# A causal attention and expert layer on one core: values held back beside projections, x laid out across, and a down product in full height

## The reference

```python
qkv = (x @ w_qkv).reshape(B, S, 3, H, D)          # H = 16 heads, D = 32
q, k, v = qkv[:, :, 0], qkv[:, :, 1], qkv[:, :, 2]
q, k = _unit_norm(q), _unit_norm(k)               # t * rsqrt(sum(t*t) + 1e-6)
q = m * _apply_rope(q, cos, sin) + (1.0 - m) * q  # m = 1 for heads 0, 2, 4, ...
k = m * _apply_rope(k, cos, sin) + (1.0 - m) * k
logits = einsum('bshd,bthd->bhst', q, k) * q_gain[None, :, None, None]
attn = softmax(where(causal, logits, finfo.min))
y = einsum('bhst,bthd->bshd', attn, v).reshape(B, S, Dm) @ w_out
x = _layernorm(x + y)
# 8 experts of width 352, the best 2 for each token, weighted by their softmax score
g = silu(einsum('td,edh->teh', x, w_gate)) * einsum('td,edh->teh', x, w_up)
routed = einsum('teh,ehd,te->td', g, w_down, comb)
shared = silu(x @ sw_gate) * (x @ sw_up) @ sw_down    # width 704
out = _layernorm(x + routed + shared)
```

## Time and profile before

| | us |
|---|---|
| median of 3 runs | 1081.23 |
| lowest and highest | 1080.83, 1082.02 |
| span of the profiled execution | 1101.7 |
| PE busy in it | 1056.5 (96%) |
| DVE, ACT, POOL busy | 623.5, 543.4, 395.7 |
| PE busy with scores L1495, values L1545 on exponents | 188.4, 136.7 |
| PE busy with projections L1445 (three parts) | 57.8, 56.2, 55.4 |
| PE busy with down products L751 on hid_h | 66.3 |

### The profile page before, as it was taken

How to read it: one execution, slowest core, us unless ns; L and a number is a source line. 1 busy time by engine, 2 the same in 40 slices (tenths; PEclk the granted TensorE clock), 3 DMA queues, 4 the chain that set the end, 5 groups by cost and what they waited for, 6 DMA issues and landing times.

```text
span 1101.7 us, 17977 instructions
## 1 busy us (share of the span) xinstructions
PE 1056.5 (96%) x6171; PEld 753.5 (68%) x6172; DVE 623.5 (57%) x1094; ACT 543.4 (49%) x900; POOL 395.7 (36%) x323
## 2 busy tenths in 40 slices
PE   7799999999999999999999996899999999999996
PEld 6654656645566466643477674589999999998885
DVE  3578694896848777687688452232222222223776
ACT  3467776687767776778645410123222222221213
POOL 2232132321224222214342177082466664623430
PEclk9999999999999999999999998799999999999999
DMA  6444514463353624346163036253444443423443
GB/s 192 131 130 136 160 63 125 129 173 96 97 143 106 182 58 116 106 129 177 48 207 110 7 147 239 88 194 103 155 155 155 131 155 102 134 85 105 125 134 115
DMA packets 106097, 141.58 MB, mean 129 GB/s; under 512 B 12784, under 2 KB 57328, under 8 KB 106032
## 3 DMA queue, kind: packets, MB, share of 16 engines
q1 hardware_dynamic: 89664, 103.22, 31.9%
q10 hardware_dynamic: 11088, 20.19, 5.3%
q0 software_dynamic: 5280, 17.31, 4.8%
HBM read 84.59 MB, written 56.10 MB: 128 GB/s over the span
## 4 chain that ended last, share of the span: by engine, by line
PE 83%; ACT 6%; DVE 5%; issue 3%; POOL 1%; another core or an unknown queue 1%; DMA 0%; SPq 0%; ACTq 0%; DVEq 0%
PE scores L630 14%; PE scores L1495 12%; PE bank L1445 12%; PE bank L1545 9%; PE scores L704 7%; PE bank L618 7%; PE bank L751 6%; ACT probs L1647 4%; PE scores L529 4%; PE bank L1542 3%; PE scores L646 2%; DVE key_sum L1768 1%; PE scores L595 1%; PE bank L1474 1%; POOL wqkv_l L1845 1%
## 5 line engine op out<-in xcount | busy, mean ns | idle before, releaser
L1647 ACT ACTIVATE probs<-scores,shift_now 128x1024 f32<-128x1024 f32 (+3 forms) x296 | 273.6, 975 | 82.4 <-PE scores L1495 64.5
L1768 DVE TENSOR_TENSOR key_sum<-key_sum,probs 128x2048 f32<-128x2048 f32 (+1 forms) x96 | 204.1, 2126 | 53.8 <-PE bank L1545 18.8
L1495 PEld LDWEIGHTS scores<-q_stack,k_stack 96*128 96x128 f32 x640 | 104.6, 190 | 137.9 <-ACT probs L1647 71.5
L1495 PE MATMUL scores<-q_stack,k_stack 96*128 96x512 f32 (+3 forms) x640 | 188.4, 405 | 3.7 <-ACT probs L1647 3.4
L1545 PE MATMUL bank<-probs,v_sb 128*32 128x512 f32 (+3 forms) x1184 | 136.7, 534 | 0.0
L630 PE MATMUL scores<-ffn_w,xt_h 128*128 (+1 forms) x608 | 127.4, 331 | 0.0
L1217 POOL TENSOR_TENSOR ffn_w<-raw,ones 128x1408 fp32r<-128x1408 f32 (+4 forms) x36 | 72.1, 2013 | 134.1 <-PE bank L618 97.0
L630 PEld LDWEIGHTS scores<-ffn_w,xt_h 128*128 128x128 f32 x608 | 99.8, 189 | 7.7 <-issue 5.5
L704 PE MATMUL scores<-x1T_h,ffn_w 128*128 128x512 f32 x352 | 92.2, 396 | 9.2 <-DVE silu L1043 6.4
L1009 DVE TENSOR_TENSOR ht_l<-scores,ht_h 128x256 fp32r<-128x256 f32 x39 | 16.6, 425 | 145.8 <-ACT ht_h L833 145.8
L1524 POOL TENSOR_SCALAR_AFFINE_SELECT probs<-probs 128x512 f32<-128x512 f32 x40 | 43.0, 1077 | 151.4 <-ACT probs L1647 151.2
(11 more groups left out here) (243 smaller groups left out, 1726.8 us busy)
## 6 DMA issues: line engine op xcount, KB each, us to landing
q_stack<-turn_scratch SPq DMA_DIRECT2D x48, 256.0 KB, 3.9
k_stack<-turn_scratch SPq DMA_DIRECT2D x48, 256.0 KB, 4.2
x_sorted<-zeros SPq DMA_DIRECT2D x39, 256.0 KB, 2.9
y_sorted<-y_tile ACTq DMA_DIRECT2D x39, 256.0 KB, 2.6
x_tile<-x_sorted ACTq DMA_DIRECT2D x37, 256.0 KB, 2.7
turn_scratch<-turned_h SPq DMA_DIRECT2D x32, 256.0 KB, 2.0
turn_scratch<-turned_l SPq DMA_DIRECT2D x32, 256.0 KB, 2.0
raw<-w_gate SPq DMA_DIRECT2D x8, 704.0 KB, 5.5
```

What stands on the lines that cost most here:

```text
L1495: mm = nc.tensor.matmul(scores[:, p, hh, lo:CH], k_stack[0:3 * HD, h, j * P:(j + 1) * P], q_stack[0:3 * HD, i % 2, h, lo:CH], start=True, ...
L1647: nc.scalar.activation(exponents(g, slot)[:, 2 * p:2 * p + 2, lo:CH], scores[:, p, :, lo:CH], ACT.Exp, bias=shift_now[:, p:p + 1]).then_in ...
L1768: nc.vector.tensor_tensor(key_sum[:, :, lo:CH], key_sum[:, :, lo:CH], probs[:, slot % 4, :, lo:CH], ALU.add).then_inc(sum_dve, 1)
```

## The change

It has four parts.

1. **x laid out across.** The host passes x a second time with the features on the partitions (`x_across`), w_qkv grouped by heads and the rotation tables by partition. x is loaded straight into `xT_raw`; the 64 transposes of x, with `pe_turn_x`, are gone. w_qkv of a group comes in one transfer of 6 KB rows in place of three of 512 B pieces. The first low part of w is made by DVE in place of POOL. The opening's projections go round three banks of PSUM and wait for the copy of the projection three before.
2. **Values held back.** In an odd slot with a projection, PE leaves out the values of the slot before and makes them in the next slot, ahead of that slot's own.
3. **Tables.** Projections, normalise, rotate, turn and stack entries are moved, and the reading of the sums of chunk 1 is no longer put inside a normalise (`SUMS_INSIDE`).
4. **Down product of half 0.** The third chunk (64 rows) has its high rows in one half of the partitions and its low rows in the other of `hid_h`. Two matmuls of 128 rows, with high weights twice and then zero over low weights, replace three of 64 rows. The weights take an extra transfer of 128 KB and an extra copy on ACT; a DVE memset stands in place of a subtraction.

```diff
-PROJECT_AT = {(0, 0): -15, (0, 1): -14, (0, 2): -13, (0, 3): -12, (1, 0): -9, (1, 1): -7, (1, 2): -4, (1, 3): -3,
...
+PROJECT_AT = {(0, 0): -13, (0, 1): -12, (0, 2): -11, (0, 3): -9, (1, 0): -7, (1, 1): -5, (1, 2): -4, (1, 3): -3,
+              (2, 0): 1, (2, 1): 2, (2, 2): 3, (2, 3): 5, (3, 0): 7, (3, 1): 9, (3, 2): 11, (3, 3): 13}
-NORMALISE_AT = {(0, 0): -12, (1, 0): -4, (2, 0): 4, (3, 0): 11}
-ROTATE_AT = {(0, 0): -11, (1, 0): -3, (2, 0): 6, (3, 0): 13}
+NORMALISE_AT = {(0, 0): -9, (1, 0): -3, (2, 0): 5, (3, 0): 13}
+ROTATE_AT = {(0, 0): -8, (1, 0): -2, (2, 0): 6, (3, 0): 15}
...
-OPENING = [("x", 0), ("x", 1), ("p", 0), ("x", 2), ("p", 1), ("x", 3), ("x", 4), ("p", 2), ("x", 5), ("x", 6),
...
+OPENING = [("p", n) for n in range(9)] + [("t", 0), ("p", 9), ("t", 1), ("p", 10), ("p", 11), ("t", 2)]
...
+def held(g, slot):
+
+    return slot % 2 == 1 and any(True for _ in work_at(PROJECT, slot, g))
...
-                mm = nc.tensor.matmul(qkv_ps[:, 0:3 * P], xs[:, k, tok], ws[:, k, :],
+                mm = nc.tensor.matmul(qkv_bank(n)[:, 0:3 * P], xs[:, k, tok], ws[:, k, :],
...
-                    if not later(g):
-                        for t in LATE_X_AT.get(slot, []):
-                            pe_turn_x(t)
+                    if held(g, slot):
+                        continue
+                    if slot and held(g, slot - 1):
+                        pe_values(g, slot - 2)
                     if slot or later(g):
                         pe_values(g if slot else g - 1, (slot - 1) % SLOTS)
...
             for k in parts:
-                k0, k1 = shared_chunks(half)[k]
-                for m, (hs, low) in enumerate(((hid_h, 0), (hid_l, 0), (hid_h, 1))):
-                    mm = nc.tensor.matmul(bank[n % 2][:], hs[k0:k1, k, tt * P:(tt + 1) * P], shared_down(half, slot, low, k),
-                                          start=(m == 0 and k == 0), stop=(m == 2 and k == 2))
+                both = half == 0 and k == 2
+                for hs, low in ((hid_h, 0), (hid_h, 1)) if both else ((hid_h, 0), (hid_l, 0), (hid_h, 1)):
+                    mm = nc.tensor.matmul(bank[n % 2][:], hs[:, k, tt * P:(tt + 1) * P], shared_down(half, slot, low, k),
+                                          start=(k == 0 and hs is hid_h and low == 0), stop=(k == 2 and low == 1))
...
-            for t in range(1, NT):
-                sp.dma_start(x_tile_in(t), x_rows[t * P:(t + 1) * P, :]).then_inc(x_loaded[t], 16)
+            for n in range(1, 6):
+                load_x(sp, n)
...
+        def dve_first_w_low():
+            nc.vector.wait_ge(w_high, 1)
+            nc.vector.tensor_tensor(wqkv_l[:], wqkv_raw[:], wqkv_h[:].bitcast(F32), ALU.subtract).then_inc(w_low, 1)
```

More of the change, by code:

```diff
@@ L1632, in act_exp @@
             lo = max(0, (j - TPC * i) * P)
-            if not later(g) and slot == 0:
-                nc.scalar.wait_ge(x_turned, EARLY)
             if later(g) or slot >= 4:
@@ L1651, in _ @@
         def _(act):
-            for kind, n in OPENING:
+            for kind, n in OPENING_HIGH:
                 if kind == "x":
```

141 lines of the change are left out of this document (65 added, 76 removed).

## The result

The changed kernel takes 1109.41 us (median of four runs, 1106.57 to 1112.68) against 1081.62 for the kernel before on the same chip (1080.83 to 1084.92). The ratio is 1.0251, with a 95% interval of 1.0226 to 1.0276: it is slower by 27.8 us, outside my range of 1072 to 1089. The profiled run took 1106.57 with a span of 1104.8. The profile of before ahead of the prediction was of an execution some 20 us longer than its median. Attention, where the change acts, reads the same in both (slot 152, where its last eight slots begin, starts at 523.8 and 524.2), so the readings of it stand.

What follows compares the result with a forecast made beforehand. The prediction took PE (TensorE) as the bound, with 83% of the chain. Gains of 30.4 us and new waits of 31.8 summed to +1.4 on 1081.23, so 1082.6 us, with a range of 1072 to 1089.

Steps and rivals of the forecast that it cites:

- A: Opening: without x's transposes and with three banks, first scores at 42.3 instead of 49.14; -8.6 us, between -5 and -11.
- B: Held values: 43 fewer changes into and out of the 32-column form on PE, 0.30 each; -12.9 us, to -17.
- C: Low part of w no longer late for the projections in the opening and at slot 25; -0.8 us.
- D: PE waits for rotated q at turn (2,0), 1.2 each, and turn (3,0), 2.4 each; +10.8 us, from 4 to 14.
- E: POOL's mask of slot 33 stands behind the k rotation; PE waits 5.6 in groups 0, 1, 2; +16.8 us, 10 to 23.
- F: Small waits for slot 9's mask, chunk 2's sums in the first group and the last group's key sum; +4.2 us, 0 to 7.
- G: Down product of shared half 0: eight matmuls a tile, 0.63 less per tile over four blocks; -8.1 us, -4 to -12.
- Rival 1: Slot 33's masks on POOL each meet another DVE addition: 22.8 us of waits, time 1088.6; chance 0.25.
- Rival 2: POOL free early, its last rotation step not slowed: mask waits fall to 10 us, time 1076; chance 0.21.
- Rival 3: Opening gives PE's full difference, 13.8 us in place of 8.6: time 1077.4; chance 0.09.
- Rival 4: Holding makes exponents on ACT late: 0.1 more per hold, 4.3 us, time 1086.9; chance 0.08.

Runs made afterwards that it cites:

- before_again: The kernel before, unchanged and profiled a second time; the run took 1086.78 us.
- xs: The kernel before with only x laid out across and the new opening; old tables, sums reading and down product, nothing held; 1075.42 us (ratio 0.9944).
- xs_hold8: xs with values held in odd slots with a projection except 25 and 27, eight a group; 1074.46 us (ratio 0.9937 to the kernel before).
- xtd_no_hold: The changed kernel with its new tables but no values held back; 1127.1 us (ratio 1.0343 to the kernel before).
- xd_only: The changed kernel with the tables of before and nothing held, leaving x across, the opening and the new down product; 1089.91 us (ratio 1.0023).
- chunk0_earlier: The changed kernel with projections, normalise, rotate and turns of the next group's chunk 0 moved earlier; 1104.72 us (ratio 1.0183 to the kernel before).
- mask_delay: xs with POOL repeating the mask of slot 33 eight times in groups 0 to 2; 1116.64 us (ratio 1.0294 to the kernel before).
- d_only: The kernel before with only the new down product of half 0; 1081.7 us (ratio 1.0004).
- d_late_b: The kernel before with the new down product and POOL's second split moved behind the scatters; 1082.61 us (ratio 0.9972).
- late_split: xds_hold8 with POOL's second split of expert weights moved behind the scatters; 1072.74 us (ratio 0.9911 to the kernel before).
- xs_h_late: xs_hold8 with POOL's second split of expert weights moved behind the scatters; 1095.43 us (ratio 1.0071 to the kernel before).
- xds_hold8: The changed kernel with old tables, sums read inside the normalise, and values held except in slots 25 and 27; 1085.52 us (ratio 0.9968 to the kernel before).
- late_b: The kernel before with only POOL's second split of expert weights moved behind the scatters; 1103.05 us (ratio 1.013).
- xd_t3: xd_only with only chunk 3's entries of the new tables; 1102.54 us (ratio 1.0143 to the kernel before).

## Why the prediction was wrong

Attention is 25.0 us worse where the sum said 9.5, and the down product gave nothing where it said 8.1. Against the 27.8 of the medians that leaves 2.8. First PE's time from the first scores to slot 152, cut in three (the extra of the half level is the estimate above, half of the time that PE is busy in it; the work is what is left of the busy time; 4.0 of after's 13.8 belong to the opening's half level, and so to A):

| | before_again | xs | xs_hold8 | xtd_no_hold | after |
|---|---|---|---|---|---|
| length | 475.1 | 473.0 | 470.9 | 511.0 | 505.7 |
| PE idle | 6.3 | 4.9 | 9.8 | 30.8 | 40.0 |
| extra of the half level | 3.0 | 4.4 | 3.9 | 12.8 | 13.8 |
| PE's work at the full level | 465.8 | 463.8 | 457.1 | 467.4 | 451.9 |

Then attention by the steps of the sum:

| step | predicted | measured |
|---|---|---|
| A opening | -8.6 | -6.8 (xd_only) |
| B held values, 43 pairs | -12.9 | -11.9 (work, xs to after; 0.28 each) |
| C w's low part | -0.8 | -0.8 |
| D turns (2,0), (3,0) | +10.8 | +8.7 (3 x 0.90, 3 x 2.01) |
| E mask behind the k rotation | +16.8 | +16.1 |
| F small waits | +4.2 | +3.0 (1.5 + 1.0 + 0.5) |
| q's transfer late | none | +6.6 |
| first scores of groups 1 to 3 | none | +1.5 |
| PE's waits for exponents | none | -0.5 |
| half clock behind the waits | none | +9.7 (estimate) |
| not accounted for | | -0.6 |
| sum | +9.5 | +25.0 |

The terms that the sum had are 1.2 lower together than forecast. What it lacked is 17.3, more than the whole miss.

**What held.** The mechanism of E is shown with its size: 5.4 a wait where I had 5.6, the step of 2.49 beside the addition, and chunk0_earlier, which moves only chunk 0, takes 9.4 of the 16.1 away. That the same tables cost 36 without holding is also shown. D is right in place and in size, F within its range, B in what it takes from PE's work. Rival 1 (each mask meets an addition too) didn't come: the masks took 0.6. Rival 2 (POOL free early) didn't either. Rival 3 is refuted by the wait of 4.86 in the opening: DVE sets its end. Rival 4 didn't come for exponents under the new tables, 2.9 against 3.4 before, but did in xs_hold8.

**The half clock, the step that failed most.** I wrote a wait as its length. I had a place in the profile of before where an idle stretch is followed by the half level and used it in A alone. In after, 24 us of attention behind the opening run at half level, in five stretches of 3.4 to 6.8: behind the wait of turn (3,0) in groups 0 and 1 (1.7 each by the estimate) and behind E's wait in groups 0, 1 and 2 (1.5 to 2.6 each). mask_delay measures such a price apart, 1.5 to 2.6 beyond each wait of 7.6. So "sum the waits" must become "sum the waits, and add 1.5 to 2.6 to each of several us".

**The wait for q's transfer** was missing altogether, six waits of up to 1.9. The transfer takes 3.9 from issue to landing in the page's list, and PE now comes sooner from a turn to the scores that use it: xtd_no_hold has the same tables and no such wait, chunk0_earlier and xs_hold8, which hold, have 6.0 and 2.1. I costed the turn's own wait, not what its stack leads to.

**B** was right as work, 0.28 a pair where I had 0.30, but wrong in "nothing hides it". Work taken out of PE brings it sooner to what it needs. Under after's tables holding takes 15.6 of work away (467.4 to 451.9), and 9.3 of it come back as idle time; in xs_hold8 it takes 6.6 away, and 5.0 come back.

**A** was short by 1.8: the first scores at 43.51 instead of 42.3, and the half level over 38 to 52 instead of 0.4 us of loss.

**G** is where reading failed beyond attention. PE's side was right: 7.41 and 7.26 for the first two blocks, 1.8 a tile. But I took the first block as on the way to routing. What is on the way is POOL and DVE: the scatters of POOL take 41.6 to 44.6 us in all profiles (most in d_only and d_late_b), and the chain to the first of them ends on a DVE cast that can't end before POOL's split. d_only measures between -1.2 and +2.2 for the whole of G. I had costed the split's queue (POOL) as having slack, not what it does to DVE.

Beyond attention, after and before_again differ little: 0.6 less to the first scatter, 0.4 less in the scatters, 4.4 less from there to the first tile, 0.3 more for the rest. With 25.0 that gives the 19.8 between the two profiled runs (1106.57 and 1086.78). The medians differ by 27.8; no profile shows where the other 8.0 lie. What varied most over the profiles is the stretch from last scatter to first tile, 8 to 36 us. Why it varies is open. It goes with the chip as much as with the kernel: it is 8 to 10 us in all four profiles of the third chip (d_only, xs, xs_hold8, late_split) and 13 to 36 in the twelve of the others named above (in the two profiles of the result it is 9.2 for after and 32.7 for before). So the place of POOL's split is not shown to be the cause of 10.2 in xs_hold8 against 35.7 in xs_h_late, nor of 22.7 in xds_hold8 against 7.9 in late_split: each pair is from two chips, and none of the four was run on both.

## What to carry to other kernels

Where one engine is busy throughout, price a wait of several microseconds above its length: look in the profile at what the granted clock does behind the waits that are already there, and add it. When PE gets faster, look again at every transfer and turn that it had just not waited for: here more than half of what holding took out came back as waits. When work moves beside another engine's, follow it to the instruction that it slows by running beside it, not only to those that wait for it: here one placement of a POOL instruction made a mask 2.0 later, another a DVE cast 2.8 later. And take the price of a change of form from rows with the same numbers of rows and columns, both before and behind.

## What the hardware showed that I had not expected

A DVE cast with a single input of 128x8 took 3.00 us beside POOL's two-input product, and 0.17 without it; a 128x512 subtraction took 2.30 in before and 0.69 in late_b, where the product stands later. The Trainium skill, GPSIMD Engine Reference, Specifications, names DVE instructions in a 2-port perf mode or with two SBUF inputs as those that contend with POOL. The subtraction has two inputs, and its rows agree; in which mode the cast ran no row shows. What the rows show of it is that it ended with POOL's product. And behind a wait of 1.2 (turn (3,0) in xd_t3) stood 3.4 us at half clock, while behind the wait of 2.01 for the same turn in group 2 of after there were none; what tells them apart these runs don't show.
